# Attention's output projection: one f32 product becomes two f32r parts, two slots later

## The reference

```
# X: (8, 512, 128); 16 heads of 64; P = X @ W_in + b_in, split into Q, K, V, G per head
d2 = q2[..., :, None] + k2[..., None, :] - 2.0 * qk
dist = jnp.sqrt(jnp.maximum(d2, 0.0))
W = jnp.power(EPS + dist, -P_POW)                       # EPS 1e-4, P_POW 2
W = W / (EPS + jnp.sum(W, axis=-1, keepdims=True))
A = jnp.einsum('hbts,hbse->hbte', W, V)
H = G * A                                               # gate
H = jnp.transpose(H, (1, 2, 0, 3)).reshape(b, t, 16 * 64)
return H @ W_out + b_out                                # the output projection (1024 -> 128)
```

## Time and profile before

| | |
|---|---|
| three runs | 1420.4, 1422.97, 1423.03 us |
| median | 1422.97 us |
| the profiled execution | 1423.09 us |
| its span | 1421.3 us |
| mean granted clock of TensorE | 0.994 |
| attention's steady part | some 60 to 890 us of the span |
| the output projection (line 451) in it | 32 times, 1.8 us each |

### The profile page before, as it was taken

One profiled execution on the slowest core, in us unless ns is written; L12 is line 12 of the kernel. 1 busy time (PEld: TensorE's weight loads), 2 busy tenths in 40 slices (PEclk: granted clock), 3 DMA queues, 4 the chain that ended last, 5 costly groups with the idle time before them and its releaser, 6 DMA issues.

```text
span 1421.3 us, 18230 instructions
## 1 busy us (share of the span) xinstructions
PE 1388.2 (98%) x6486; PEld 743.3 (52%) x6486; DVE 1091.0 (77%) x2046; ACT 1100.7 (77%) x951; POOL 840.3 (59%) x657
## 2 busy tenths in 40 slices
PE   8999999999999999999999999899999999999996
PEld 5444444444443444444444444445777777777675
DVE  7887887888888887887888778635677686776857
ACT  2799889979978979979979979944676776776752
POOL 4568777778778778868877876411333433333330
PEclk9999999999999999999999999999999999999999
DMA  3000110101101101101101012442011010110100
GB/s 113 1 17 17 24 46 17 23 25 38 24 17 46 24 17 33 37 17 31 39 16 32 16 30 61 115 142 106 1 68 60 8 68 1 68 60 8 68 1 15
DMA packets 45705, 54.99 MB, mean 39 GB/s; under 512 B 13808, under 2 KB 32368, under 8 KB 44464
## 3 DMA queue, kind: packets, MB, share of 16 engines
q1 hardware_dynamic: 45616, 53.84, 12.6%
HBM read 48.97 MB, written 4.85 MB: 38 GB/s over the span
## 4 chain that ended last, share of the span: by engine, by line
PE 86%; DVE 8%; ACT 5%; issue 1%; DMA 0%; DVEq 0%; SPq 0%; ACTq 0%
PE sc L406 14%; PE av L419 13%; PE z L74 12%; PE pj L74 12%; PE y L1221 8%; PE sc L401 6%; PE y L74 5%; PE pj L383 4%; PE pj L451 4%; DVE w L597 3%; PE pj L429 2%; ACT w L684 1%; ACT w L688 1%; ACT w L680 1%; DVE high L565 1%
## 5 line engine op out<-in xcount | busy, mean ns | idle before, releaser
L597 DVE TENSOR_SCALAR w<-sc 128x1024 f32<-128x1024 f32 x256 | 301.2, 1217 | 70.0 <-PE sc L406 68.9
L680 ACT ACTIVATE w<-w 128x2048 f32<-128x2048 f32 x128 | 237.5, 1904 | 123.6 <-DVE w L597 123.2
L320 POOL TENSOR_TENSOR wsum<-wsum,w 128x512 f32<-128x512 f32 x248 | 317.9, 1282 | 19.4
L969 POOL TENSOR_TENSOR hr_l<-hr,hr_h 128x512 fp32r<-128x512 f32 x112 | 151.9, 1356 | 263.1 <-ACT hr L1025 263.1
L406 PE MATMUL sc<-query,key 64*128 64x512 f32 x1024 | 243.1, 594 | 0.0
L684 ACT ACTIVATE w<-w 128x2048 f32<-128x2048 f32 x128 | 240.1, 1899 | 0.4
L688 ACT ACTIVATE w<-w 128x2048 f32<-128x2048 f32 x128 | 239.8, 1897 | 0.0
L419 PE MATMUL av<-w,vt 128*64 128x512 f32 x1024 | 233.8, 598 | 2.6 <-ACT w L688 2.5
L1025 ACT ACTIVATE hr<-z,b 128x512 f32<-128x512 f32 x256 | 173.4, 684 | 67.7 <-PE z L74 67.6
L306 POOL TENSOR_TENSOR sqq<-query 128x512 f32<-128x512 f32 x63 | 65.6, 1042 | 187.6 <-DVE query L537 147.4
L317 POOL TENSOR_TENSOR wsum<-w 128x512 f32<-128x512 f32 x124 | 159.4, 1285 | 5.2 <-ACT w L688 5.2
(11 more groups left out here) (215 smaller groups left out, 2362.5 us busy)
## 6 DMA issues: line engine op xcount, KB each, us to landing
hT<-head_recips SPq DMA_DIRECT2D x64, 256.0 KB, 3.9
rb<-routing SPq DMA_DIRECT2D x8, 2048.0 KB, 6.9
w<-in_W SPq DMA_DIRECT2D x16, 256.0 KB, 4.8
xa<-in_X SPq DMA_DIRECT2D x8, 256.0 KB, 4.5
xc<-in_X SPq DMA_DIRECT2D x8, 256.0 KB, 2.7
x<-xc SPq DMA_DIRECT2D x8, 256.0 KB, 3.9
x<-x SPq DMA_DIRECT2D x1, 1792.0 KB, 7.9
out<-prod SPq DMA_DIRECT2D x7, 256.0 KB, 2.3
```

Source lines behind the costliest of these rows:

```text
L320: nc.gpsimd.tensor_tensor(wsum[:, u, :], wsum[:, u, :], w[:, j % 2, u, c, :], ALU.add).then_inc(s_added, 1)
L597: nc.vector.tensor_scalar(w[:, s, 2 * r:2 * r + 2, c, :], sc[:, i, :, :], 0.0, None, ALU.max).then_inc(s_d2, 1)
L680: nc.scalar.activation(w[:, j % 2, u, :, :], w[:, j % 2, u, :, :], ACT.Sqrt).then_inc(s_sqrt, 1)
```

## The change

The output projection is done by f32r parts. `wout` is split once into `wout_h` and `wout_l` (ScalarE's cast at the head of period 1, GpSimd's subtraction in its loop's j = 1). Of each `hT` ScalarE makes the high part `hT_h` (`high_part(j-3)`, between the square roots of units 1 and 2), and GpSimd the low part `hT_l` (`low_part(j-4)`, between the squares of head pair 0 and pair 1). The output projection of period j-4 stands in slot 2, behind G0 and G1, instead of that of j-3 in slot 1; VectorE's addition to `oT` follows it. `turn_output` and `add_output` go to slot 3 of group 3. `normalize(j-2)` stands at the end of GpSimd's loop, which is the same place in its stream as the head of the next turn. The input `xs` and the keys' rows `krow` have one buffer instead of two. At the seam to the experts, four output projections are placed anew among the experts' steps, the split of `w2` begins four steps later, and the broadcast of the routing weights is made in two pieces.

```diff
-        xs = [sb("xh", [P, 2, T], F32R), sb("xl", [P, 2, T], F32R)]
+        xs = [sb("xh", [P, T], F32R), sb("xl", [P, T], F32R)]
-        krow = sb("krow", [P, 2, 2, T], F32R)
+        krow = sb("krow", [P, 2, T], F32R)
...
-            if k == 1 and 0 <= j - 3 < NQ:
-                names.append(("out", j - 3))
-            if k == 2 and q == 2 and b >= 1:
+            if k == 2 and 0 <= j - 4 < NQ:
+                names.append(("out", j - 4))
+            if k == 3 and q == 3 and b >= 1:
                 names.append(("out_t", b - 1))
...
+            def low_part(j):
+                pool.wait_ge(s_hT_h, j + 1)
+                nc.gpsimd.tensor_tensor(hT_l[:, j % 2, :, :], hT[:, j % 2, :, :], hT_h[:, :, :].bitcast(F32),
+                                        ALU.subtract).then_inc(s_hT_l, 1)
+            def last_parts(j):
+                pool.wait_ge(s_hT, j + 1)
+                pool.wait_ge(s_pj, use["out", j - 1] + 1)
+                nc.gpsimd.tensor_copy(hT_h[:, :, :], hT[:, j % 2, :, :]).then_inc(s_hT_h, 1)
+                low_part(j)
             for j in range(-1, NQ):
-                if 0 <= j - 3 < NQ:
-                    normalize(j - 3)
                 if j + 1 < NQ:
                     squares(j + 1, 0)
+                    if 0 <= j - 4:
+                        low_part(j - 4)
                     if j >= 0:
                         squares(j + 1, 1)
...
+                if j == 1:
+                    pool.wait_ge(s_wout, 1)
+                    nc.gpsimd.tensor_tensor(wout[1][:, :, :], wout_f[:, :, :], wout[0][:, :, :].bitcast(F32),
+                                            ALU.subtract).then_inc(s_wout, 1)
...
                 if j == 0:
-                    pe.wait_ge(s_late_in, 16 * N_LATE)
-                if j == NQ - 3:
-                    fill(nc, pj[:, n, :], ident, 4)
-                pe.wait_ge(s_hT, j + 1)
+                    pe.wait_ge(s_wout, 2)
+                pe.wait_ge(s_hT_l, j + 1)
                 for r in range(2):
-                    m = nc.tensor.matmul(pj[:, n, :], wout[:, 2 * (j % QUADS) + r, :], hT[:, j % 2, r, :],
-                                         start=(r == 0), stop=(r == 1))
+                    m = product(nc, pj[:, n, :], [w[:, 2 * (j % QUADS) + r, :] for w in wout],
+                                [hT_h[:, r, :], hT_l[:, j % 2, r, :]], start=(r == 0), stop=(r == 1))
...
+            def high_part(j):
+                act.wait_ge(s_hT, j + 1)
+                if j >= 1:
+                    act.wait_ge(s_pj, use["out", j - 1] + 1)
+                nc.scalar.copy(hT_h[:, :, :], hT[:, j % 2, :, :]).then_inc(s_hT_h, 1)
             def square_roots(j):
                 for u in range(4):
                     r, v = divmod(u, 2)
+                    if u == 2 and j >= 3:
+                        high_part(j - 3)
...
+                if j == 1:
+                    act.wait_ge(s_late_in, 16 * N_LATE)
+                    nc.scalar.copy(wout[0][:, :, :], wout_f[:, :, :]).then_inc(s_wout, 1)
                 weights(j)
...
-                if (b, k) == (0, 7):
+                if (b, k) == (0, 4):
+                    output(NQ - 3)
+                if (b, k) == (0, 10):
                     output(NQ - 2)
-                if (b, k) == (0, 16):
+                if (b, k) == (0, 19):
                     output(NQ - 1)
-                if (b, k) == (0, 18):
+                if (b, k) == (0, 22):
                     turn_output(B - 1)
...
-                if b == 0 and k >= 24:
+                if 28 <= n < 28 + NE:
```

More of the change, by code:

```diff
@@ L132, in build_attention @@
         w = sb("w", [P, 2, 4, NC, T])
-        wout = sb("wout", [P, PAIRS, D])
+        wout_h = sb("wout_h", [P, PAIRS, D], F32R)
+        with ExitStack() as until_split:
+            wout_f = until_split.enter_context(nc.sbuf_tensor("wout", [P, PAIRS, D], F32))
+        wout = [wout_h, sb("wout_l", [P, PAIRS, D], F32R)]
         bqkg = sb("bqkg", [P, PAIRS, 3])
@@ L138, in build_attention @@
         gT = sb("gT", [P, PAIRS, T])
-        hT = sb("hT", [P, 2, 2, T])
+        with ExitStack() as until_split:
+            hT = until_split.enter_context(nc.sbuf_tensor("hT", [P, 2, 2, T], F32))
+        hT_l = sb("hT_l", [P, 2, 2, T], F32R)
+        hT_h = sb("hT_h", [P, 2, T], F32R)
         vt = sb("vt", [P, NC, H0 * E0])
@@ L191, in build_attention @@
         N_LATE = 3
-        PERIODS = range(-1, NQ + 3)
+        PERIODS = range(-1, NQ + 4)
         SLOTS = 4
@@ L269, in normalizer @@
                 sp.wait_ge(s_rec_out, 16 * (j + 1))
+                if j >= 2:
+                    sp.wait_ge(s_pj, use["out", j - 2] + 1)
                 for v in range(2):
@@ L281, in sync @@
                 b, q = divmod(j, QUADS)
-                if q == 0 and b >= 1:
+                if q == 2 and b >= 1:
                     store_x1(b - 1)
@@ L363, in values @@
                     pe.wait_ge(s_rest_l, 2)
-                product(nc, pj[:, bank(("v", b, n)), :], [x[:, b % 2, c * P:(c + 1) * P] for x in xs],
+                product(nc, pj[:, bank(("v", b, n)), :], [x[:, c * P:(c + 1) * P] for x in xs],
                         [v[:, h * T:(h + 1) * T] for v in wv]).then_inc(s_pj, 1)
@@ L475, in step @@
                         values(b, n)
-                if k == 1 and 0 <= j - 3 < NQ:
-                    output(j - 3)
-                if k == 2 and q == 2 and b >= 1:
-                    turn_output(b - 1)
+                if k == 2 and 0 <= j - 4 < NQ:
+                    output(j - 4)
                 if k == 2 and q == 2 and b + 1 < B:
@@ L486, in step @@
                     weighted_values(j - 1, 1)
+                if k == 3 and q == 3 and b >= 1:
+                    turn_output(b - 1)
                 if k == 3 and q == 0 and 1 <= b < B:
@@ L585, in key_rows @@
                     dve.wait_ge(s_high, 4 * j + 2 * r + 2)
-                    nc.vector.scalar_tensor_tensor(krow[:, j % 2, r, :], source, row[:, r, 3:4], high[:, :].bitcast(F32),
+                    nc.vector.scalar_tensor_tensor(krow[:, r, :], source, row[:, r, 3:4], high[:, :].bitcast(F32),
                                                    ALU.mult, ALU.subtract).then_inc((s_high, s_pj_free)[r], 1)
@@ L648, in step @@
                         norm_stats(b + 1)
-                if k == 1 and 0 <= j - 3 < NQ:
-                    output(j - 3)
-                if k == 2 and q == 2 and b >= 1:
-                    add_output(b - 1)
+                if k == 2 and 0 <= j - 4 < NQ:
+                    output(j - 4)
                 if k == 2 and 0 <= j - 2 < NQ:
@@ L660, in step @@
                     weighted_values(j - 1, 1)
+                if k == 3 and q == 3 and b >= 1:
+                    add_output(b - 1)
                 if k == 3 and q == 0 and 1 <= b < B:
@@ L1212, in expert @@
                     pe.wait_ge(S["rwT"], 1)
-                if n == NU + 1:
-                    pe.wait_ge(S["w2s"], NE * NF)
+                if b == 1 and i == 1:
+                    pe.wait_ge(S["w2s"], NF * (k // NF + 1))
                 pe.wait_ge(S["hr"], n + 1)
@@ L1295, in _ @@
             sums(NQ - 2)
-            output(NQ - 3)
             turn_f(0)
@@ L1304, in _ @@
                     weighted_values(NQ - 1, 0)
+                if n == 4:
+                    output(NQ - 4)
                 hidden(n)
@@ L1579, in step @@
                     sums(NQ - 1)
+                if (b, k) == (0, 5):
+                    output(NQ - 3)
+                if (b, k) == (0, 4):
                     for e in range(5, NE):
```

72 lines of the change are left out of this document (45 added, 27 removed).

## The result

| | before | changed |
|---|---|---|
| median of six runs | 1421.91 us | 1461.37 us |
| lowest to highest | 1420.40 to 1423.03 | 1459.36 to 1467.86 |
| the profiled execution | 1423.09, span 1421.3 | 1459.36, span 1457.6 |
| mean granted clock of the profiled execution | 0.994 | 0.987 |

The ratio is 1.028, its 95% interval 1.0268 to 1.0292: the change made the kernel slower by 39.5 us. I had forecast +24, so the direction was right, the size too small, and the time lies just outside the range.

The account below looks back on a forecast made before the run. TensorE's work sets the period, the ring through ScalarE 0.67 behind; the change makes the ring bind. Terms 9.4 - 2.3 + 0.2 + 12.6 + 1.0 - 0.4 + 3.6 = +24.1 on 1423.1 gave 1447 us, range 1430 to 1461.

Parts of the forecast that it names:

- the ring through exponential 1: Plain period: ScalarE's square roots to exponential 1, TensorE's weighted values to the next root; 25.33 against the period's 26.00.
- +0.72 per plain period: Projection in slot 2 lengthens the ring to 26.72 from a 26.00 period; 13 plain links, +9.4.
- about -0.3 where the values are projected: Links from group 0 to 1: only TensorE's work counts, seven links at -0.33, -2.3.
- The argument from period 2: Without an output projection, weighted values start right behind exponential 1 and the period is 26.38; offered as evidence for the order.
- Group 2, +12.6 forecast: Six links from group 1 to group 2, each +2.1 with the low part blocking VectorE's train on xa.
- the clock falls: Rival: TensorE's waits in group 2 and at the seam bring stretches at the lower clock; +12, 1459, chance 0.14.
- the blocking: Group 2: GpSimd's low part holds up VectorE's four instructions on xa, lasting some 3.9 instead of 1.59.
- The +0.2: Group 1 to 2 link if the train isn't blocked: longer slot 2 alone, 14.24 + 0.06 + 12.68 + 0.78 = 27.76.
- The seam, +3.6 forecast: Seam and experts: cast, moved projections, routing weights' wait and GpSimd's last parts, summed to +3.6.
- The train on `xn_f`: Seam: GpSimd's casts and subtractions of the last parts fall on a VectorE train; +1.0, bounds 0 and 2.4.
- the wait at the first weighted values of the seam: Sign named beforehand: at the seam this TensorE wait should be over 3 us; it was 1.66 before.
- The rival of TensorE's work alone: Rival: the ring is not closed, so 32 projections save 0.33 each; -10.6, 1412.5, chance 0.09.

Follow-up runs that it names:

- e7: Changed kernel plus nine unused small products in TensorE's group 2 wait, batches 1 to 6 only; 1451.95 us (1.0214).
- e1: Changed kernel with GpSimd's low part of hT moved behind the squares of pair 1; 1441.7 us (1.0138).
- e9: Changed kernel: projection in slot 1, low part before pair 0's squares, wout's low part at j = 2, GpSimd's seam work behind VectorE's trains; 1414.8 us (0.9950).
- e10: Same as e9 but without moving wout's low part to GpSimd's j = 2; 1419.0 us (0.9977).

## Why the prediction was right and where it was wrong

The reading of the bound was right: TensorE at 98% was not bound by its own work alone, the ring through exponential 1 stood 0.67 us behind. Both terms that rest on it were right, +0.72 per plain period to the hundredth and about -0.3 where the values are projected. Four kernels show it: the ring with 1.39 or 1.81 more in slot 2 (26.72, 27.05), with nothing more in it (25.68), and 1.8 shorter (25.7). The argument from period 2 was weaker than it reads: that period is of group 2, with the turning of the next input in slot 2, so its 26.38 cannot be held against a plain period, and TensorE waited only 0.12 for the exponential there. That ScalarE's cast, the buffers, and GpSimd's low part in a plain period cost nothing was right as well.

Two terms of the sum were too small. The step that failed in both is the clock: the prediction priced the waits that the change makes on TensorE, and its sum held nothing for the lower clock behind them. At the seam the wait itself was put too short as well.

*Group 2, +12.6 forecast, +21.3 measured.* The mechanism was right, down to the train (3.9 forecast, 3.69 measured), and the one link at full clock cost 2.03 where 2.1 stood. What failed was to have set "the clock falls" as a rival of its own, with 0.14, beside the blocking, so that the term of 2.1 a link held nothing for it. It follows from the blocking: the waits of 2.12 and 0.54 that it makes are followed by a clock of 0.50 in five of six places, and with these waits filled or gone (e7, e1) the clock stays up in all six. The links so come to 3.5 more on average, not 2.1. I had argued that the waits were short pieces, from the 1.66 us at 893.45 after which the clock had stayed up; this row spoke for a shorter wait than the one I was forecasting. The nine fillers give back 9.4 us, which is this part of the error (21.3 - 12.6 = 8.7). One step of the working doesn't add up: 1.39 - 0.4 + 0.5 gives 1.49 for slot 2, where the sum has 0.78. The +0.2 that came of it is near what e1_low_late shows, 27.61 against 27.46, but not by its own terms.

*The seam, +3.6 forecast, +7.1 measured.* The routing weights' wait was right (1.9 and 1.92). The train on `xn_f` was put at +1.0, with 2.4 as its bound: I had let one GpSimd instruction meet the train, where the order has normalisation, cast and subtraction in a row. It cost 3.36 of waiting, and the clock at 0.83 behind it. Holding back the last parts alone gives back 4.5. One of the signs named beforehand didn't come: the wait at the first weighted values of the seam is 1.91, not over 3. The other terms of the seam were not measured one by one.

The smaller terms: at the start `wout`'s low part cost 2.7 of waiting, with a clock of 0.50 from 76 to 79 behind it, and 3.3 of the link to period 2, not the 1.0 I took from between 0 and 3.4; earlier links, from the first table load on, were shorter by as much in these executions, so the sum hid it, and e9 and e10 showed it. That each group's last link would carry turn_output's 0.6 when the ring no longer hides it, I had not priced, since in the changed kernel it is hidden.

The rival of TensorE's work alone (1412.5) was wrong of this change. The same idea comes near its number when the projection stays ahead of the weighted values and GpSimd's instructions lie clear of VectorE's trains: 1413.5 to 1414.8. That the numbers meet is in part luck: in e9's profile attention is 10.4 ahead of the kernel before at the table load of period 30, and 3.4 of it are lost again behind that.

## What to carry to other kernels

A busy share of 98% doesn't say that an engine is the bound by its own work: look at the two timelines and measure the ring that runs through the other engine, since work moved from outside the ring into it costs its full length less the ring's slack (here 1.39 - 0.67 = 0.72 a period), even when it has become shorter. A new GpSimd instruction in a gap of GpSimd's was free here only where VectorE had no run of SBUF-to-SBUF instructions at that time. And a wait forecast on TensorE is to be priced together with the clock behind it, not as an alternative to it.

## What the hardware showed that I had not expected

- VectorE's four instructions of 128x128 (SBUF to SBUF, f32) last 1.11 us alone, 1.59 beside one GpSimd square, 3.69 beside a square and the low part, 5.43 and 6.14 beside three GpSimd instructions in a row. A run gets one instruction in between two of GpSimd's: each blocked one ends 0.08 or 0.09 behind the end of a GpSimd instruction (at 424.89 and 427.25 behind 424.81 and 427.16 in group 2; at 986.62, 987.72 and 990.14 behind 986.54, 987.64 and 990.06 at the seam). The Trainium skill has the rule of the shared pair of ports ("SBUF — State Buffer", "Who interferes with whom"), by which the engine that comes second is blocked for the whole of the other's instruction, and these numbers agree with it.
- Waits of TensorE of 2.12 and 0.54 us (once 0.43), 0.5 apart, were followed by some three microseconds at half the clock in four places and by some seven in one, and by no fall in a sixth; 0.54 alone was followed by none in any of six (e1_low_late, e7_fill_9), and neither was 1.66.
- Products of two heads of 64 columns that alternate take 3.65 us for sixteen records, in blocks of one head 5.42. The Trainium skill's page "TensorE: Matmul & The Clock Gate", section "Part 3: Packing small matmuls — row/col tiling", has products on different parts of the array run at the same time; that the order of issue decides it is what this run shows.
